# Two low planes over copied rows, statistics by lane swap, two banks of sums and later outputs in a grouped 7x7 dynamic convolution

## The reference

```python
x = x + conv3x3(sign(group_norm(x)), sign(w)) * scale      # 32 groups of 2 channels
v = group_norm(x)
r = relu(batch_norm(w_r @ v + b_r))                        # 64 -> 16 channels, per pixel
ker = w_s @ r + b_s                                        # 16 -> 49 * 16, per pixel
for ki in range(7):
    for kj in range(7):                                    # 16 groups of 4 channels
        out += pad(v)[:, :, :, ki:ki+56, kj:kj+56] * ker[:, :, ki * 7 + kj][:, :, None]
x = x + out
```

## Time and profile before

| what | value |
|---|---|
| median of 3 runs | 2095.22 us (2088.94 to 2097.33) |
| the profiled execution | 2100.36 us |
| its span | 2097.7 us, mean granted clock of PE 0.914 |
| busy DVE, ACT, POOL | 1350.2, 1056.1, 1025.0 us |
| DMA | 436.47 MB, mean 208 GB/s; queue q1 (SP) 73.7%, q10 (ACT) 9.8% of 16 engines' span |

### The profile page before, as it was taken

The page is one execution under the profiler, slowest core; times in us unless marked ns, Lnnn a source line. Parts: engine busy times, 40 slices in busy tenths (PEclk is TensorE's granted clock), DMA queues, the critical chain, the costliest instruction groups (busy, mean ns, idle before and its releaser), DMA issues.

```text
span 2097.7 us, 39368 instructions
## 1 busy us (share of the span) xinstructions
PE 1703.9 (81%) x15168; PEld 752.8 (36%) x15168; DVE 1350.2 (64%) x1652; ACT 1056.1 (50%) x758; POOL 1025.0 (49%) x905
## 2 busy tenths in 40 slices
PE   3487887888788788887878888788887878878775
PEld 2243333433333333333333333333333433333332
DVE  5376665757667575776657667576766757667574
ACT  2354555544555445555545555445555545554453
POOL 2145455444545444555454545445555454544573
PEclk8798999999989899999989999899998999989997
DMA  4679789797898978899797997978799798997894
GB/s 102 171 184 225 202 229 227 183 232 198 223 210 206 230 192 222 199 236 238 185 234 185 236 225 200 227 195 229 194 233 230 190 228 198 235 225 185 211 259 110
DMA packets 224283, 436.47 MB, mean 208 GB/s; under 512 B 89214, under 2 KB 136751, under 8 KB 219951
## 3 DMA queue, kind: packets, MB, share of 16 engines
q1 hardware_dynamic: 148832, 382.57, 73.7%
q10 hardware_dynamic: 75264, 51.39, 9.8%
HBM read 336.06 MB, written 84.93 MB: 201 GB/s over the span
## 4 chain that ended last, share of the span: by engine, by line
issue 38%; POOL 37%; PE 9%; SPq 7%; DMA 3%; DVE 2%; ACT 2%; POOLq 0%; ACTq 0%; DVEq 0%
POOL folded L369 37%; SPq L307 5%; PE ybank L564 3%; PE ybank L583 2%; DMA patches<-parts_dram 2%; PE obank L594 1%; DVE prod L820 1%; SPq L289 1%; DMA relu<-blocks 1%; PE ybank L554 1%; PE ybank L525 1%; PE obank L601 1%; PE ybank L615 1%; ACT blocks L458 0%; ACT blocks L416 0%
## 5 line engine op out<-in xcount | busy, mean ns | idle before, releaser
L369 POOL TENSOR_TENSOR folded<-prod 128x448 f32<-128x448 f32 x896 | 1013.3, 1144 | 1051.0 <-DVE prod L820 1040.6
L820 DVE TENSOR_TENSOR prod<-ybank,relu 128x896 f32<-128x896 f32 x896 | 956.8, 1086 | 314.2 <-PE ybank L583 240.2
L583 PE MATMUL ybank<-patches,wspan 128*64 128x448 f16 x7168 | 845.5, 374 | 157.2 <-DVE prod L820 128.5
L436 ACT ACTIVATE patches<-patches 64x1792 f16<-64x1792 f16 x448 | 740.9, 1698 | 450.0 <-DMA patches<-parts_dram 228.5
L583 PEld LDWEIGHTS ybank<-patches,wspan 128*64 128x64 f16 x7168 | 370.5, 114 | 657.7 <-DVE prod L820 256.8
L594 PE MATMUL obank<-patches,wbias 128*32 128x448 f16 x3584 | 223.4, 399 | 80.1 <-ACT osb L424 80.1
L601 PE MATMUL obank<-folded,esum 128*32 128x448 f32 x1792 | 225.7, 577 | 1.5 <-POOL folded L369 1.5
L525 PE MATMUL ybank<-sgn,convw 128*128 128x448 bf16 x1008 | 207.3, 359 | 12.7 <-ACT sgn L389 7.6
L594 PEld LDWEIGHTS obank<-patches,wbias 128*32 128x32 f16 x3584 | 93.3, 105 | 199.0 <-ACT osb L424 95.7
L832 DVE TENSOR_TENSOR xs<-ybank,xs 128x1024 f32<-128x1024 f32 (+1 forms) x64 | 61.9, 967 | 142.1 <-PE ybank L615 142.1
L615 PE MATMUL ybank<-back,blocks 128*128 128x128 f32 (+1 forms) x448 | 70.5, 310 | 101.1 <-ACT blocks L458 101.1
(11 more groups left out here) (92 smaller groups left out, 447.3 us busy)
## 6 DMA issues: line engine op xcount, KB each, us to landing
patches<-parts_dram SPq DMA_DIRECT2D x1232, 224.0 KB, 6.4
parts_dram<-parts SPq DMA_DIRECT2D x128, 256.0 KB, 3.4
xs<-x_dram SPq DMA_DIRECT2D x128, 196.0 KB, 4.7
sums_dram<-osb ACTq DMA_DIRECT2D x112, 224.0 KB, 5.7
rows<-sums_dram ACTq DMA_DIRECT2D x112, 224.0 KB, 5.0
out_dram<-xs SPq DMA_DIRECT2D x128, 196.0 KB, 3.7
relu<-blocks SPq DMA_DIRECT2D x256, 49.0 KB
patches<-gb_dram SPq DMA_DIRECT2D x1, 784.0 KB
```

Source lines behind the costliest of these rows:

```text
L369: pool.tensor_tensor(folded[:, u % 8, :], prod[:, u % 2, 0, :], prod[:, u % 2, 1, :], ALU.add).then_inc(fold_done, 1)
L436: act.activation(X2[0:COPIED_ROWS, e % 2, at], X1[0:COPIED_ROWS, e % 3, at], ACT.Copy).then_inc(copied, 1)
L583: mm = pe.matmul(bank("unit", p, n)[64 * t:64 * t + 64, h, 0:N], wspan[0:STACK_ROWS[stack], stack, g, h, :], of_group(e, stack, g), start= ...
L820: dve.tensor_tensor(prod[:, u % 2].rearrange("m h (n c) -> m h n c", c=GC), bank("unit", p, n)[:, :, 0:N].rearrange("m h (n c) -> m h n c" ...
```

## The change

1. **Planes.** `X2` now takes five planes by copy and two by DMA. `copy_high` copies all 128 partitions of a piece of `X1` to `X2` instead of 64; the two low planes that come by DMA are laid over copied rows (rows 3, 7, ... and 66, 70, ...). So `second_stack(e)` waits until all four pieces of strip e are copied, and no longer for the readers of the buffer, which the copies wait for. Pieces are copied at units 0, 1, 2, 3 of a strip, no longer at 0, 1, 4, 5. On SP `first_stack(e + 2)` stands ahead of `second_stack(e + 1)`, and at the start `spread(0)` ahead of `second_stack(0)`. The memset of `X2` is gone.
2. **Statistics.** `gmat`, `Mbank` and the three matmuls a pair are gone. DVE swaps neighbouring lanes with `stream_shuffle` and adds. The variance is computed right after unit 18, the root at 18, the affine at 20, the normalisation at 21; the sign is at 5.
3. **Sums.** `Obank` is two banks, strip by strip. The bias of strip e waits for the `gather` of strip e-2, no longer of e-1.
4. **Outputs.** The first output additions of a pair go from units 46 and 49 to 50 and 53, their `arrange` from 43 to 46.

```diff
-PLANES = (((0, 0, 0, 4), (0, 4, 64, 4), (0, 1, 1, 4), (1, 0, 65, 4),
-           (0, 2, 2, 4), (1, 1, 66, 4), (0, 3, 3, 4), (1, 2, 67, 4)),
-          tuple((0, a, a, 4) for a in range(4)) + ((0, 4, 64, 4), (1, 3, 65, 4), (1, 4, 66, 4)))
+PLANES = (((0, 0, 0, 4), (0, 3, 64, 4), (0, 1, 1, 4), (0, 4, 65, 4),
+           (0, 2, 2, 4), (1, 1, 66, 4), (1, 0, 3, 4), (1, 2, 67, 4)),
+          ((0, 0, 0, 4), (0, 3, 64, 4), (0, 1, 1, 4), (0, 4, 65, 4),
+           (0, 2, 2, 4), (1, 4, 66, 4), (1, 3, 3, 4)))
-COPIED_ROWS, COPIED_PLANES = 64, 4
+COPIED_PLANES = 5
-FIRSTLOAD, SECONDLOAD = 16 * 8, 16 * 3
+FIRSTLOAD, SECONDLOAD = 16 * 8, 16 * 2
-STAT0_AT, MEAN_AT = 7, 5
+MEAN_AT, SIGN_AT = 4, 5
-STAT1_AT, STAT2_AT = 21, 23
-GROUP_AT, VARIANCE_AT, AFFINE_AT = 19, 21, 22
+VARIANCE_AT, AFFINE_AT = 18, 20
+ROOT_AT, NORMAL_AT = 18, 21
-OUT0_AT = {46: 0, 49: 1}
-ARRANGE1_AT, ARRANGE0_AT = 13, 43
+OUT0_AT = {50: 0, 53: 1}
+ARRANGE1_AT, ARRANGE0_AT = 13, 46
-COPY_AT = {0: 0, 1: 1, 4: 2, 5: 3}
+COPY_AT = {0: 0, 1: 1, 2: 2, 3: 3}
...
             def second_stack(e):
+                sp.wait_ge(copied, JX * (e + 1))
                 if e >= 2:
-                    sp.wait_ge(y_ready, GP * (e - 1))
                     sp.wait_ge(second_in[e % 2], SECONDLOAD * (e // 2))
...
             first_stack(0)
+            spread(0)
             second_stack(0)
-            spread(0)
             first_stack(1)
             for p in range(pairs):
                 for s in range(E):
                     e = E * p + s
+                    if e + 2 < EALL:
+                        first_stack(e + 2)
                     if e + 1 < EALL:
                         second_stack(e + 1)
-                    if e + 2 < EALL:
-                        first_stack(e + 2)
...
-                act.activation(osb[:], Obank[:, 0:N], ACT.Copy, scale=alpha[:]).then_inc(o_read, 1)
+                act.activation(osb[:], Obank[e % 2][:, 0:N], ACT.Copy, scale=alpha[:]).then_inc(o_read, 1)
...
-                act.activation(X2[0:COPIED_ROWS, e % 2, at], X1[0:COPIED_ROWS, e % 3, at],
-                               ACT.Copy).then_inc(copied, 1)
+                act.activation(X2[:, e % 2, at], X1[:, e % 3, at], ACT.Copy).then_inc(copied, 1)
...
             def bias(e, stack):
-                if stack == 0 and e > 0:
-                    pe.wait_ge(o_read, e)
+                if stack == 0 and e >= 2:
+                    pe.wait_ge(o_read, e - 1)
...
             def negative_mean(p):
-                dve.wait_ge(stat_ready, 3 * p + 1)
-                dve.tensor_scalar(col(S_NMEAN), Mbank[:, 0:1], -1.0 / HW, None, ALU.mult).then_inc(stat_read, 1)
-                dve.wait_ge(stat_read, 3 * p + 1)
-                dve.tensor_copy(col(12), col(S_NMEAN)).then_inc(nmean_ready, 1)
+                link(dve.stream_shuffle(other[:, 0:1], col(S_SUM), OTHER))
+                link(dve.tensor_tensor(both[:, 0:1], col(S_SUM), other[:, 0:1], ALU.add))
+                dve.tensor_scalar(col(S_NMEAN), both[:, 0:1], -0.5 / HW, None, ALU.mult).then_inc(nmean_ready, 1)
...
+            def variance(p):
+                link(dve.stream_shuffle(other, mv[:], OTHER))
+                link(dve.tensor_tensor(both, mv[:], other, ALU.add))
+                link(dve.tensor_tensor(col(S_D), mv[:, 0:1], other[:, 0:1], ALU.subtract))
                 link(dve.tensor_tensor(col(S_U), col(S_D), col(S_D), ALU.mult))
+                link(dve.tensor_scalar(col(S_T), both[:, 1:2], 0.5, EPS, ALU.mult, ALU.add))
+                link(dve.tensor_scalar(col(S_GM), both[:, 0:1], 0.5, None, ALU.mult))
+                link(dve.tensor_scalar(col(S_U), col(S_U), 0.25, None, ALU.mult))
+                dve.tensor_tensor(col(S_VE), col(S_T), col(S_U), ALU.add).then_inc(var_ready, 1)
```

More of the change, by code:

```diff
@@ L19 @@
 HALVES, OH = 2, 8
+OTHER = [i ^ 1 for i in range(32)]
 K, PAD = 7, 3
@@ L150, in build @@
         Ybank = [ctx.enter_context(nc.psum_tensor(f"ybank{i}", [128, 2, 512], F32)) for i in range(3)]
-        Obank = ctx.enter_context(nc.psum_tensor("obank", [128, 512], F32))
-        Mbank = ctx.enter_context(nc.psum_tensor("mbank", [128, 512], F32))
+        Obank = [ctx.enter_context(nc.psum_tensor(f"obank{i}", [128, 512], F32)) for i in range(2)]
         D = nc.dram_tensor("parts_dram", (2, 2, 128, PART), F16, kind="Internal").ap()
@@ L244, in build @@
         (S_SUM, S_NMEAN, S_GM, S_D, S_T, S_VE, S_SD, S_Y, S_U, S_RS, S_NB) = range(11)
+        other, both = sm[:, 30:32], sm[:, 32:34]
         def cols(i, n):
@@ L486, in _ @@
                         rows(e - 1)
-                    if more and n == STAT0_AT:
+                    if more and n == SIGN_AT:
                         sign(p + 1)
-                    if more and n == STAT2_AT:
+                    if more and n == ROOT_AT:
                         root(p + 1)
+                    if more and n == NORMAL_AT:
                         normalize(p + 1)
@@ L505, in turn @@
                     pe.wait_ge(*read_by(*TURNS[i - 3]))
-            def stat(p, n):
-                if n == 0:
-                    pe.wait_ge(sum_ready, p + 1)
-                    rhs = col(S_SUM)
-                else:
-                    pe.wait_ge(stats_ready, 2 * p + n)
-                    rhs = mv[:, 0:1] if n == 1 else col(S_T)
-                if 3 * p + n > 0:
-                    pe.wait_ge(stat_read, 3 * p + n)
-                pe.matmul(Mbank[:, 0:1], gmat[:], rhs, start=True, stop=True).then_inc(stat_ready, 1)
             def conv(p, k):
@@ L541, in select_bias @@
                     sel, n = t_sel16[:, pos], 32 * pos
[L542 to L544 removed]
+                    pe.matmul(Obank[0][:, n:n + 16], sel[:, 0, :], t_b16[:, 0, :], start=True, stop=True)
+                    pe.matmul(Obank[0][:, n + 16:n + 32], sel[:, 1, :], t_b16[:, 0, :], start=True, stop=False)
+                    mm = pe.matmul(Obank[0][:, n + 16:n + 32], sel[:, 2, :], t_b16[:, 1, :], start=False, stop=True)
                 mm.then_inc(bsel_ready, 1)
@@ L569, in of_group @@
                 at = (X1[:, e % 3, :], X2[:, e % 2, :])[stack]
-                return at[0:STACK_ROWS[stack]].rearrange("k (j g n) -> k g j n", g=GROUPS, n=8)[:, g]
+                return at.rearrange("k (j g n) -> k g j n", g=GROUPS, n=8)[:, g]
             def taps(p, n):
@@ L593, in bias @@
                         g = 4 * t + i
-                        pe.matmul(Obank[32 * t:32 * t + 32, 0:N], wbias[0:STACK_ROWS[stack], stack, g, :],
+                        pe.matmul(Obank[e % 2][32 * t:32 * t + 32, 0:N], wbias[:, stack, g, :],
                                   of_group(e, stack, g), start=(stack == 0 and i == 0), stop=False)
@@ L617, in outputs @@
                 mm.then_inc(out_ready, 1)
-            pe.wait_ge(first_loaded, FIRST_LOADS)
-            stat(0, 0)
             pe.wait_ge(convw_ready, 2)
@@ L623, in _ @@
                 conv(0, k)
-            stat(0, 1)
-            stat(0, 2)
             pe.wait_ge(taps_ready, 1)
@@ L648, in _ @@
                         sums(e, 0)
-                    if more and n == STAT0_AT:
-                        stat(p + 1, 0)
                     if more and n in CONV_AT:
@@ L654, in _ @@
                         outputs(p - 1, 2 + OUT1_AT[n])
-                    if more and n == STAT1_AT:
-                        stat(p + 1, 1)
-                    if more and n == STAT2_AT:
-                        stat(p + 1, 2)
                     if more and n in T_AT:
```

46 lines of the change are left out of this document (9 added, 37 removed).

## The result

The changed kernel takes 2149.14 us (median of 4 runs, 2133.80 to 2150.71); the one before took 2092.84 us on the same chip. The ratio is 1.0252, with a 95% interval of 1.0208 to 1.0296: slower, by 2.5%. Forecast were 2120 and a chance of 0.51 for slower.

What follows compares the result with a forecast made beforehand. Bound by waits between engines (PE 81% busy), and by DMA at 239 GB/s where many planes are wanted. A pair's terms sum to +1.1, times 15 +17, once +8: 2125 from 2100.4, median 2120; range 2052 to 2166.

Steps and rivals of the forecast that it cites:

- S to T6: End of the spread's issue to strip 6's first matmul: 13.5 us against 8.7, +4.8, second stack behind eight planes.
- R1: Rival, chance 0.27: the two planes do not queue behind the eight, strip 6 starts after 9.9 us; faster, median 2049.
- T6 to T0: Strip 6's first matmul to the next pair's first: copies, gather and two planes' landing take 14.5 us, -0.2.
- T0 to T1: First matmul of strip 0 to that of strip 1: DVE carries it, 12.3 us, equal, taken as -0.3.
- T1 to T2: First matmul of strip 1 to that of strip 2: PE stays full, two stat matmuls go, -0.4 us.
- T2 to T4: First matmul of strip 2 to that of strip 4: earlier variance, then DMA ends it, 33.3 us against 36.1, -2.8.
- T4 to S: First matmul of strip 4 to the end of the spread's issue: 18.5 + 12.2 us, unchanged.
- the frame: The prediction's account of a pair, called wrong if the spread starts sooner than 18.5 us behind strip 4's first matmul.
- Once: Costs outside the repeated pairs: start +4 and -1, last pair +5, together +8 us.
- R2: Rival, chance 0.17: loss equals gain, ACT's two transfers lie outside the stretch before strip 6, 11.6 us; median 2091.
- R3: Rival, chance 0.16: ACT's loop, with three copies, binds light strips, 1.64 us more in each; slower, priced 2155.

Runs made afterwards that it cites:

- e8: The changed kernel with the eight planes of each pair's first strip moved by half, same number of issues; 2095.86 us, ratio 0.9984 to the kernel before.
- e1: The changed kernel with strip 6's second stack issued ahead of the next pair's eight planes, in strip 5 only; 2124.28 us, ratio 1.0137.
- e4: The changed kernel with the planes part put back as before (three planes by DMA, 64 partitions copied, old units and order); 2018.39 us, ratio 0.9618.
- e3: The kernel before with the planes part of the change alone; 2224.48 us, ratio 1.0601.
- e10: The kernel of e4 with only the four copies moved to units 0, 1, 2, 3; 2039.38 us, ratio 0.9714.
- e9: The changed kernel with the second stack's two planes issued by ScalarE behind its fourth copy, none by SyncE; 2148.07 us, ratio 1.0249.
- e13: The kernel of e9 with SyncE waiting for the present strip's two planes before issuing eight for the strip after next; 2084.23 us, ratio 0.9922.

## Why the prediction was right, and where its sizes were off

*S to T6* (forecast 13.5, measured 14.7, and 14.6 over the pairs). The step that makes the kernel slower was named with its place, its releaser and its order. That it is bytes in a queue is shown by e8 (the bytes), e1 (the order) and e4 (without them 6.0). The bounds were 9.9 and 16.6. The size is in part luck, for the bytes were not those of my sum. The stretch in the trace (start and end, us, busy of PE, PEld, DVE, ACT, POOL, clock, DMA share, GB/s):

```profile
959.88:974.58 14.70, 0.00 (x1) 0.03 (x1) 0.00 (x0) 3.88 (x3) 0.56 (x1) 0.64 0.95 216
```

That is 3.2 MB at 216 GB/s, where I had 2.75 MB at 239 and 2.0 us. By the packets of its queues only one of ACT's two transfers moved in it (0.23 MB), but SyncE's queue brought 12.3 planes instead of ten: some of the eight issued behind the two moved beside them. The stretch of before that gave the 2.0 us had the same in it (12.5 planes where I counted 11, one transfer of ACT), so the 2.0 us are not simply a time from issue to data.

PE stood 15.8 us where I had written some 10, since units 46 and 47 were done before S. By the Trainium skill (DMA: Bandwidth & Descriptors, "Queues, rings and completion order"), against R1, a DMA's increment lands only behind the earlier writes of its engine; the 14.7 agrees.

*T6 to T0* (14.5, 15.1). The chain stood as described, but not the clock. TensorE had stood 15.77 us, and its first 24 matmuls took 3.89 instead of the 2.46 at 1057.95. The granted clock was low for these 24, mostly at 1.2 GHz (a mean of 0.63), and 1.00 right behind them:

```profile
974.58:978.50 3.92, 3.92 (x25) 2.13 (x26) 1.84 (x2) 2.68 (x2) 1.01 (x1) 0.63 1.03 257
978.40:981.30 2.90, 2.90 (x28) 1.49 (x28) 2.90 (x4) 0.00 (x0) 2.46 (x3) 1.00 0.42 103
```

From T6 to the end of the eight sums behind unit 51 it is 6.7 us, between my 5.3 for the full clock and 7.5 for half. The Trainium skill's sentence that the throttled clock is the default (TensorE: Matmul & The Clock Gate, "What's actually happening") holds for the start. The price was 1.4 us, not the 2.2 between my 13.4 and 15.6, since the clock was back at 1.00 by 978.4. The gather then began 0.1 behind the sums, where I had 0.8. What made the step longer than 14.5 is the issue and the landing: the two issues took 1.91, not 1.3, and T0 is 989.65 - 986.05 = 3.6 behind their end, not 3.3. Over the pairs it went from 15.8 to 15.5, -0.3 where I had -0.2.

*T0 to T1* (-0.3) and *T1 to T2* (-0.4): over the 14 pairs 12.5 to 12.6 and 22.7 to 21.7, +0.1 and -1.1.

*T2 to T4* (forecast 33.3, from a mean of 36.1): 34.0 in this pair, 33.2 in the one before:

```profile
896.81 1.71 PE L569 MATMUL ybank<-patches,wspan 128*64 128x448 f16 x16
...
930.04 2.46 PE L569 MATMUL ybank<-patches,wspan 128*64 128x448 f16 x24 [1.94 <-DMA patches<-parts_dram]
```

Over the pairs the two strips fall from 35.8 to 33.6, -2.2 against -2.8. That the transfers of planes end them, not the statistics, is right: both rows wait for patches, and in e4, with the planes back, the two strips are 30.6. But the small net term hides two larger ones that my sum did not have apart: the planes alone lengthen the two strips by 3.3 (e3), and the rest shortens them by 5.2 to 5.5.

*T4 to S* (unchanged): 29.9 against 30.8. The spread started 17.9 behind T4, where I had written that sooner than 18.5 would break the frame. It was off by 0.6 in this pair; over the 15 pairs it is 18.5 on average (18.8 in before), and T4 to S went from 31.1 to 30.4.

*The sum.* A pair is +1.8, not +1.1; over 14 of them 25.0 instead of 15. By terms it is +5.9, -0.3, +0.1, -1.1, -2.2, -0.6 for +4.8, -0.2, -0.3, -0.4, -2.8, 0: errors of both signs that cancel in part. The split shows more of that luck. The terms that belong to the planes come to some +78 (15 x 4.6, and 9 once), the others, with all of T2 to T4, to some -54; measured were +130 and -76. Both were too small, by 40 and 29%, and the misses of 52 and -22 leave 30 in the whole. *Once* was forecast at +8. The start cost nothing (-0.9 against +3): the copies start at 77.67 and the second stack is hidden as well. From the last S to the end it is +10.3: from the last pair's T0 to the end it is 115.4 instead of 111.3 (+4, forecast +5), and the rest, some 6, is that pair's own S to T0 (28.9 against 22.7), which my sum had put into the fifteenth pair.

*From the trace to the median.* For an execution like the profiled one I had 2125, and the profiled one was 2133.8. Then I took off 5, since before's trace was that much above its median; after's turned out 15 below its own. So of the 29 us between 2120 and 2149, 9 are terms, 5 are this correction and 15 are the place of the profiled execution among the others.

*The rivals.* R1 (the planes do not queue) needed T6 within 10 us of S: it came at 14.7, and e8 excludes it. R2 needed ACT's two transfers out of the stretch: one was (the sums, issued at 953.66, 6 us ahead of S), the other was in it (`rows`, issued at 963.79). Its 11.6 did not come all the same, since planes from behind and a rate below 239 filled the time. R3 is real but small: e10 shows its mechanism at 21 us, and T0 to T1 was 13.7 in this pair, on the edge of the 14 that I had set and the longest of pairs 1 to 15. Its number (2155) is nearer to the median than mine, but it wanted strip 0 1.64 longer in every pair, and on average that strip grew by 0.1; what grew is S to T6, where the forecast put it. Two edits were rightly put at about nothing (outputs, banks). The one at -2.8 a pair, the statistics, carries most of the 76 us that all but the planes win, which are 5.0 a pair.

## What to carry to other kernels

When a load is replaced by a copy, count what the copy now stands behind: 112 loads fewer moved less data, and the two that stayed had to wait for the copies and for eight planes issued ahead. A load wanted next and issued behind one wanted later paid here for most of the latter's bytes at the full rate (e8), and another queue did not help while the engines were full (e9); a wait in the issuing engine's program may be what keeps the backlog small (e9 against e13). A net term of two effects of opposite sign looks small and safe; price the two apart. Split a change of several parts before accepting or rejecting it: this one holds a part worth -76 us and one worth +130.

## What the runs showed of the hardware that I had not expected

**A small add of VectorE lasts as long as GpSimd's big one beside it.** It shows at the lane swap's adds, which are on one or two columns. VectorE and GpSimd in strip 2, then the adds by line (times, mean ns), the swap itself last:

```profile
902.83 1.09 DVE L791 TENSOR_TENSOR prod<-ybank,relu 128x896 f32<-128x896 f32 x1
904.00 1.13 POOL L366 TENSOR_TENSOR folded<-prod 128x448 f32<-128x448 f32 x1 [1.62 <-DVE prod L791]
904.03 1.12 DVE L760 TENSOR_TENSOR small<-mv,small 128x2 f32<-128x2 f32 x1
905.19 0.16 DVE L761 TENSOR_TENSOR small<-mv,small 128x1 f32<-128x1 f32 x1
```

```profile
L741 DVE TENSOR_TENSOR small<-small 128x1 f32<-128x1 f32 x16 | 16.9, 1058 | 0.5
L760 DVE TENSOR_TENSOR small<-mv,small 128x2 f32<-128x2 f32 x16 | 16.9, 1056 | 0.5
L759 DVE STREAM_SHUFFLE small<-mv 128x2 f32<-128x2 f32 x16 | 2.4, 152 | 0.0
```

The add at 904.03 takes 1.12 us and ends 0.02 behind GpSimd's; the next, of the same kind, takes 0.16. At L741 and L760 alike, 15 of the 16 began beside an add of GpSimd, took 1.11 to 1.12 us and ended 15 to 18 ns behind it; the sixteenth, at the start, where GpSimd adds nothing, took 0.16. A product in the affine (L656) is held in the same way, 0.46 us in 14 of 16 cases. Instructions with one input in SBUF are not held: the reduction ahead of L741 takes 0.21 beside GpSimd and alone, and the products of a unit, which read PSUM and SBUF, take 1.09 either way. What the two engines share was not tested by itself. Before has it too: there the same product (L680) takes 1.12 in 15 of 16 cases. So each of the two lane swaps of a pair is followed by one add of 1.12 us, which I had at 0.2.

**The cost of a landing is the backlog.** Two planes land 3.6 us behind the issue's end in after (989.65) and 3.7 in e13, with no other planes ahead of them. They land 8.1 behind it with eight planes ahead in the same queue (974.58 - 966.45, after), and 9.0 behind it with some seven planes of another queue and two transfers of sums still to move, at 236 GB/s (e9).
